# A fused attention and feed-forward kernel: key projections as pairs of half-row products, and new orders on every engine

## What is computed

```python
q = jnp.einsum('btc,hcd->bhtd', x, Wq)      # x after a layer norm
k = jnp.einsum('btc,hcd->bhtd', x, Wk)
v = jnp.einsum('btc,hcd->bhtd', x, Wv)
scores = jnp.einsum('bhtd,bhsd->bhts', q, k) * scale + bias[None]
scores = jnp.where(causal[None, None], scores, jnp.float32(-jnp.inf))
w = jax.nn.softmax(scores, axis=-1)
out = jnp.einsum('bhts,bhsd->bhtd', w, v)
...
x = x + _layernorm(attention(_layernorm(x)) )          # out @ Wp + bp
x = x + _layernorm(ffn(_layernorm(x)))
# ffn: r = sigmoid(xr @ W_r.T), k = relu(xk @ W_k.T)**2, r * (k @ W_v.T);
# xr and xk mix a token with the one before it
```

## Time and profile before

| | |
|---|---|
| median of 3 runs | 2222.81 us (2222.11 to 2223.51) |
| span of the profiled execution | 2224.4 us |
| the profiled execution beside the runs | 2224.4 us, 1.6 above their median |
| busy: TensorE, VectorE, GpSimd, ScalarE | 2111.2, 1945.6, 1697.1, 1685.6 us |
| rounds with a full tail | n = 10 to 61 |

### The profile page before, as it was taken

How to read it: one execution, slowest core, us unless ns; L and a number is a source line. 1 busy time by engine, 2 the same in 40 slices (tenths; PEclk the granted TensorE clock), 3 DMA queues, 4 the chain that set the end, 5 groups by cost and what they waited for, 6 DMA issues and landing times. The chain is left out here.

```text
span 2224.4 us, 75124 instructions
## 1 busy us (share of the span) xinstructions
PE 2111.2 (95%) x29456; PEld 1432.2 (64%) x29456; DVE 1945.6 (87%) x5210; ACT 1685.6 (76%) x2529; POOL 1697.1 (76%) x1372
## 2 busy tenths in 40 slices
PE   3798889999999999999999999999999999999986
PEld 1355556666676666667766666776666676666665
DVE  6777778999999999999999999999999998888857
ACT  2478788777878877887787788778877878877734
POOL 4376777788888888888888888888888887777752
PEclk9899999999999999999999999999999999999988
DMA  7111112232322323232232333223232322212251
GB/s 176 30 50 45 41 44 67 53 76 70 74 61 63 71 57 74 71 74 61 64 71 55 75 71 74 61 65 70 56 74 70 75 59 57 59 50 67 66 110 42
DMA packets 336784, 147.13 MB, mean 66 GB/s; under 512 B 172976, under 2 KB 335664, under 8 KB 336432
## 3 DMA queue, kind: packets, MB, share of 16 engines
q1 hardware_dynamic: 336432, 142.33, 26.9%
HBM read 24.25 MB, written 43.06 MB: 30 GB/s over the span
## 5 line engine op out<-in xcount | busy, mean ns | idle before, releaser
L1736 POOL TENSOR_TENSOR probs<-probs_f,probs 128x1024 f16<-128x1024 f32 (+3 forms) x704 | 1121.0, 1602 | 340.4 <-ACT probs L1002 338.0
L984 ACT ACTIVATE probs_f<-score_ps,score_unit 128x1024 f32<-128x1024 f32 (+3 forms) x704 | 620.6, 882 | 240.0 <-DVE score_ps L1293 114.9
L1277 DVE TENSOR_REDUCE row_max<-max_ps 128x2 f32<-128x1024 f32 (+2 forms) x640 | 632.4, 1005 | 17.2 <-PE max_ps L692 14.3
L1002 ACT CAST probs<-probs_f 128x1024 f16<-128x1024 f32 (+3 forms) x704 | 566.9, 814 | 12.3
L726 PEld LDWEIGHTS misc<-v_pair,probs 128*128 128x128 f16 x4608 | 415.0, 97 | 40.0 <-issue 29.1
L726 PE MATMUL misc<-v_pair,probs 128*128 128x65 f16 x4608 | 438.5, 194 | 0.6 <-issue 0.6
L727 PE MATMUL misc<-v_pair,probs 128*128 128x64 f16 x4608 | 436.8, 193 | 0.0
L728 PE MATMUL misc<-v_pair,probs 128*128 128x65 f16 x4608 | 435.9, 193 | 0.0
L728 PEld LDWEIGHTS misc<-v_pair,probs 128*128 128x128 f16 x4608 | 418.0, 97 | 0.0
L727 PEld LDWEIGHTS misc<-v_pair,probs 128*128 128x128 f16 x4608 | 417.9, 98 | 0.0
L616 PE MATMUL misc<-xT,w_split 128*128 128x512 f16 x1536 | 370.5, 385 | 7.2 <-DVE w_split L1396 3.8
(11 more groups left out here) (182 smaller groups left out, 3650.1 us busy)
## 6 DMA issues: line engine op xcount, KB each, us to landing
v_pair<-v_calc SPq DMA_DIRECT2D x64, 516.0 KB, 3.6
o_scratch<-o_stage SPq DMA_DIRECT2D x128, 256.0 KB, 2.5
xh<-x SPq DMA_DIRECT2D x56, 128.0 KB, 2.1
x_res<-x SPq DMA_DIRECT2D x56, 128.0 KB, 3.2
out<-out_sb SPq DMA_DIRECT2D x56, 128.0 KB, 1.7
shift_all<-shift_row SPq DMA_DIRECT2D x256, 1.0 KB
probs<-wqkv SPq DMA_DIRECT2D x1, 3072.0 KB, 13.2
probs<-band_scratch SPq DMA_DIRECT2D x8, 144.0 KB, 6.5
```

The source lines that it names most:

```text
L984: nc.scalar.activation(dst, score_ps[t % 2][:, :, 0:width], ACT.Exp, scale=score_unit[:]).then_inc(exp_done, 1)
L1002: nc.scalar.copy(dst, src).then_inc(hi_done, 1)
L1277: last = dve.tensor_reduce(dst[:, :, i % 4:i % 4 + 1], max_ps[:, :, col:col + width], AX.X, ALU.max)
L1736: pool.tensor_tensor(low, copy_of(par + ahead, t)[:, 0:2 * width], high, ALU.subtract).then_inc(lo_done_pool, 1)
```

## The change

1. k0 and k1 are no longer two `project_qk`. A new `project_pair` makes both at once in two parts. In part 0 the upper 64 rows of the contraction work on the first half of the tokens and the lower 64 on the second half, into the two banks; in part 1 they are changed over. Fill 6 stands between the parts. Both results are complete only at the end of part 1.
2. `TASKS` has new banks and a new order, and with them the waits of `opened`.
3. The order of the calls is new on all five engines. On TensorE v1 goes ahead of the keys, o1 behind s9, and s11 and s0 of the next pair behind rk and the transpose.
4. Some waits and the setup's steps (the splits of the weights, the reductions for Wp) move to other places at the start.

```diff
-TASKS = [("o2", 1, "prev"), ("o3", 0, "prev"), ("q0", 0, "qkv"), ("ffn", 1, "ffn"), ("o0", 1, "att"),
-         ("q1", 0, "qkv"), ("v0", 1, "qkv"), ("o1", 0, "att"), ("k0", 1, "qkv"), ("k1", 0, "qkv"), ("v1", 1, "qkv"),
-         ("x2t", 0, "mix"), ("proj", 1, "proj"), ("rk", 0, "mix")]
+TASKS = [("o2", 1, "prev"), ("o3", 0, "prev"), ("q0", 1, "qkv"), ("ffn", 0, "ffn"), ("o0", 0, "att"),
+         ("q1", 1, "qkv"), ("v0", 0, "qkv"), ("v1", 1, "qkv"), ("k0", 1, "qkv"), ("k1", 0, "qkv"),
+         ("o1", 1, "att"), ("x2t", 0, "mix"), ("proj", 1, "proj"), ("rk", 0, "mix")]
...
+            def project_pair(name, part, n, pair, ring, span):
+
+                which = "qk".index(name)
+                if part == 0:
...
+                    for half in range(2):
+                        opened(f"{name}{half}", n, span)
+                else:
+                    pe.wait_ge(pair_half[name], 2 * (n + LEAD + 1))
+                step = 0
+                for k in range(KT):
+                    for w, a in ((0, 0), (1, 0), (0, 1)):
+                        for r in range(2):
+                            half, rows = r ^ part, slice(D * r, D * r + D)
+                            last = pe.matmul(misc[BANK[f"{name}{half}"]][:], w_split[rows, w, which, k, bass.ds(pair, P)],
+                                             xT[rows, a, k, bass.ds(ring + half * 512, 512)],
+                                             start=part == 0 and step == 0, stop=part == 1 and step == 3 * KT - 1)
+                            if step == 3 * KT - 1:
+                                last.then_inc(full[f"{name}{half}"] if part else pair_half[name], 1)
+                        step += 1
...
+                    if has["qkv"]:
+                        project_v("v1", n, 4 * par + 2, pair // 2 * 2 * P, ring, span)
...
                     if has["qkv"]:
-                        project_qk("k0", n, pair * P, ring, span)
-                        project_qk("k1", n, pair * P, ring, span)
+                        project_pair("k", 0, n, pair * P, ring, span)
                     if has["next"]:
                         fill(m, par, 6, at)
                     if has["qkv"]:
-                        project_v("v1", n, 4 * par + 2, pair // 2 * 2 * P, ring, span)
+                        project_pair("k", 1, n, pair * P, ring, span)
+                    if has["att"]:
+                        score(m, par, 0, 8, at)
+                    if has["next"]:
+                        fill(m, par, 7, at)
                     if has["att"]:
                         score(m, par, 0, 9, at)
+                        weigh_values(1, m, par, 0, span)
+                    if has["next"]:
+                        fill(m, par, 8, at)
+                    if has["att"]:
                         score(m, par, 0, 10, at)
```

More of the change, by code:

```diff
@@ L481, in transpose_head @@
                 held(x_lo, g - NB + 1)
-                held(full[LAST_PROJECTION], n + LEAD)
+                for name in LAST_PROJECTIONS:
+                    held(full[name], n + LEAD)
                 col = g % (RING // P) * P
@@ L527, in body @@
                     n = 2 * m + par
+                    if has["xt"] and n > -LEAD:
+                        load_head(n + HEAD_LEAD)
                     if has["att"]:
                         load_shift(m, par, 0, 1)
-                    if has["xt"] and (not isinstance(m, int) or n > -LEAD):
-                        load_head(n + HEAD_LEAD)
+                    if has["proj"]:
+                        load_outputs(n, par, at)
+                        load_residual(n - PROJ_LAG)
+                    if has["next"] and par == 1:
+                        load_values(m, par)
                     if has["next"] and par == 0:
@@ L849, in body @@
                         transpose_maxima(1, n)
+                    if has["att"]:
+                        score(m, par, 0, 11, at)
+                    if has["next"]:
+                        score(m, par, 1, 0, at)
                 rolled(pe, span, body)
@@ L1098, in body @@
                         exponential(m, par, 0, 10)
+                        high_outputs(0, m, par, 0)
+                    if has["next"]:
+                        shift(m, par, 1, 1)
+                    if has["att"]:
                         exponential(m, par, 0, 11)
@@ L1101, in body @@
                         high_probs(m, par, 0, 11)
-                    if has["next"]:
-                        shift(m, par, 1, 1)
                     if has["mix"]:
@@ L1611, in body @@
                         root_step("y", n - PROJ_LAG, 6)
-                    if has["ffn"]:
-                        root_step("z", n - FFN_LAG, 7)
-                    if has["proj"]:
                         root_step("y", n - PROJ_LAG, 7)
@@ L1816, in body @@
                     if has["att"]:
+                        low_probs(m, par, 0, 7)
                         low_probs(m, par, 0, 8)
```

286 lines of the change are left out of this document (140 added, 146 removed).

## The result

| | before | after |
|---|---|---|
| median of the runs (4 each, side by side) | 2222.46 us | 2242.22 us |
| span of the profiled execution | 2224.4 us | 2239.5 us |

A forecast was written before the change was run, and what follows sets the result against it. TensorE's own pace was taken to bound 52 steady rounds, waits between engines the early ones. Steady 13, early 6, rounds 8 and 9 0.5, start 2.5 and end 0 sum to 22 us: 2201 us, 8-in-10 range 2189 to 2217.

The forecast's parts named there:

- SP: SP's new issue order: shift rows queue behind the next head's load, first read by s4 10.8 us into the round; cost 0.
- Borders: TensorE, steady round: four fewer changes between full-row and half-row products at 0.096 us each, 0.384 us saved.
- VectorE: Steady round: VectorE makes f8 and o1 late by 0.13 us, leaving 0.25 saved per round, 13 us over 52.
- Rival 1: VectorE takes the place as bound, steady rounds stay at 32.2 to 32.34 us; 2208 to 2221, say 2214; chance 0.20.
- the sum of the ledger: VectorE's work between f4's end and f8's start: 9.4 us, 9.5 with hand-overs, in 9.5 us; no slack.
- x2t to rk: Tail of the round: the steps from x2t to rk need near 2.7 us of 2.89; no cost taken, tightest spot.
- the halves side by side: Key products on TensorE: 24 half-row products run as 12 pairs, 2.60 us as before; the product itself brings nothing.
- Rivals 2 and 3: 2: rk waits for ScalarE's copy of x2t, 2245 us, chance 0.07; 3: key halves don't run together, 2360, chance 0.02.
- The slower case: Whole kernel slower by more than 0.2% (4.4 us): chance 0.09, from 0.07 and 0.02.
- Rounds 0 to 7: Early rounds without tail work go from 30.85 to 30.1 us each, 6 us saved (0 to 11).
- Start: Setup's splits and reductions stand earlier, behind q0, so the first pair's f1 starts sooner: 2.5 us saved (0 to 5).
- End: Last round: s11 later by 1.9 us, x2t somewhat sooner, closing unchanged; 0 with 2 us either way.

The follow-up runs named there:

- 2: Changed kernel with only the second half's shift rows issued at the end of the round before, ahead of the head's transpose: 2221.09 us, ratio 0.9995.
- 9: On top of 8, the values' copy is SP's first issue in even rounds: 2204.86 us, ratio 0.9914.
- 8: Changed kernel with shift rows ahead and the setup's splits and reductions back behind the first pair's projections: 2214.55 us, ratio 0.9967.
- 6: Two Newton steps fewer per root, in the kernel before (2210.68 us, ratio 0.9938) and the changed one with shift rows ahead (2189.44 us, 0.9842).
- 11: On top of 9, full-row k0, fill 6, full-row k1 instead of the key pair: 2216.64 us, ratio 0.9974.
- 5: Changed kernel with GpSimd's band scalings waiting until VectorE's three splits are done: 2230.98 us, ratio 1.0051.
- 12: Changed kernel with shift rows ahead, values' copy first in even rounds and band scalings behind the splits, setup in its own place: 2203.36 us, ratio 0.9913.

## Why the prediction was wrong

**SP, the step that failed.** "I take 0; if GpSimd were 4 us later than that, s4 would wait for them." GpSimd was where I put it (4.6 us into the round for "some 5"). I counted the head's load alone between it and the shift rows. But the same low part lets go the head's transposing transfer, and two stores and the output's store stand in the queue behind it: with the head's load 4.6 us of issues, then 1.25 for the rows' own, and 1.1 until s4 starts. The 6 us of slack that I saw were used up by SP itself. The same step missed the values' copy, moved behind a transposing transfer of 2 to 3 us. Undone, they brought 21 us (2) and 10 to 12 (9 against 8), where the sum had 0.

**Borders: right.** 0.40 a round for 0.384 with VectorE relieved (6), and 0.42 in the rounds without a head (11). Against the kernel before, the changed one saves 0.31 in these last rounds (32.03 for 32.34).

**VectorE: right in kind, too small.** I took 0.13 us of lateness a round; it is 0.26. So an undisturbed round saves 0.14 and not 0.25: 52 of them 7 us for the 13. With SP's waits gone (9) rounds 11 to 61 took 9.8 us less than before, since before they had stray waits too (32.45 on average for the undisturbed 32.34). Rival 1 was the nearer one for the steady rounds, and the sum of the ledger (9.4 us of 9.5) should have been read as a bound, not as a fit.

**x2t to rk, and the halves side by side: right.** Rivals 2 and 3 didn't come. The slower case came from a mechanism that I had named and priced at nothing.

**Rounds 0 to 7: too much.** 6 us were forecast (0 to 11) and 1.0 came. The waits for the exponentials shrank by 15.7 us, but 16.6 came at the closing transposes of these rounds, for whose maxima the forecast has no term. The trace has two smaller causes beside it: in 8 these rounds take 242.4 us, 4.4 less than before, and of the 3.4 that lie between 8 and the changed kernel 2.7 are busy time of TensorE (220.88 for 218.18, mean granted clock 0.94 for 0.95); the rest, 0.7, is of the size of the 1.1 us of waits for shift rows there.

**Start: wrong sign.** 2.5 us less were forecast, 3.1 more came. I took 6.09 us for the splits from a place where GpSimd was nearly done with its bands, and put it beside both of them. Relieved (5), the start gave 7.0 us less than before.

**End: not foreseen.** I took 0 with 2 us either way; it was 8.8 less. Round 62 gave 2 of them (28.5 us for 30.5). In the rest TensorE waits less for the last transfers (3.5 us for 6.8 in the lists of waits), and its granted clock was higher, 0.95 for 0.88, with 5.5 us less of busy time. As the trace of before is of an execution some 3.7 us above its median, part of the 8.8 may belong to that execution and not to the change. How much, no run tells apart.

With both of SP's waits gone and the setup back (9), the kernel stands at 2204.9 us, inside the range. That is in part luck. Against the trace of before it has 9.8 us less in rounds 11 to 61 (forecast 13), 1.4 in rounds 8 to 10, 0.4 in 0 to 7 (6), 1.9 at the start (2.5, though with the setup in its old place), and 7.9 in the closing, where I had put 0. The sum is 21.4 for my 22, but a third of it is the closing, which I hadn't foreseen and for which the clock is a cause that wasn't ruled out.

## What to carry to other kernels

When a step is moved ahead in a queue that issues in order, list everything that the same event releases ahead of each transfer that is needed soon, add up the issue times, and compare the landing with the first reader: a queue that spends most of a round waiting can still be late for one row. Look also for who waits to overwrite what a moved copy reads. A duration may be carried to another place only with the work of its neighbours there. And if a ledger of the second engine comes out at its full length, price the lateness from rows of that engine, or take it as the bound.

## What the runs showed of the hardware

**VectorE and GpSimd exclude each other.** The three splits of the changed kernel one by one: the timeline cut behind the first, and the line's durations (min/median/max in ns, first and last start in us):

```profile
36.08 7.10 DVE L1433 SCALAR_TENSOR_TENSOR w_split<-probs,w_scale,w_split 128x1536 f16<-128x1536 f32 x1 [0.78 <-ACT w_split L1068]
```
```profile
L1433 DVE SCALAR_TENSOR_TENSOR w_split<-probs,w_scale,w_split x3: 1806/7099/8922, 36.1 to 51.9; 128x1536 f16<-128x1536 f32 x3
```

The first ends at 43.18, 0.96 us behind the end of GpSimd's first scaling (42.22). The second took 8.92, from 43.10 to 52.02, 0.94 behind the end of the second scaling (51.08). The third, alone, took 1.81. That second scaling took 8.85 instead of 8.03, as if it had let the first split finish. It is the Trainium skill's rule, page SBUF — State Buffer, section Who interferes with whom: a VectorE instruction with two inputs in SBUF contends with a GpSimd instruction that reads SBUF, and the lock is exclusive. The trace agrees, with 17.67 us against 5.28 without the neighbour. But only 0.95 of the 1.81 us of a split lie behind the other's end, so the trace doesn't show that nothing of it was done before. Had the rule been weighed, the forecast of the start would have had a reason for the other sign.

**One order, two prices.** The same order of SP's issues cost 21 us in one kernel and 151 in the other, where 31.7 us are the same products of TensorE taking longer at a lower mean clock. The borders between full-row and half-row products cost 0.10 us each, as read from single steps, in a whole round too.

**The granted clock differs from trace to trace.** With the same order of TensorE's list, rounds 0 to 7 took 242.4, 246.4 and 249.1 us at mean granted clocks of 0.95, 0.94 and 0.92 (8, 9 and 12). A difference of some us between two traces, in a stretch where the clock isn't 1.00 throughout, says little of the change.
